# A transformer block on one core: the key and query stacks of groups 1 to 3 put together through DRAM

## What is computed

```python
q = (src @ Wq + bq).reshape(B, T, 16, 8)          # 16 heads of 8 dimensions
k = (src @ Wk + bk).reshape(B, T, 16, 8)
v = (src @ Wv + bv).reshape(B, T, 16, 8)
scores = einsum('bqhd,bkhd->bhqk', q, k) * 8 ** -0.5
probs = softmax(scores)
attn = einsum('bhqk,bkhd->bqhd', probs, v).reshape(B, T, 128) @ Wo + bo
x = layer_norm(src + attn)
# then: each token goes to one of 4 experts by its router key, and a second layer norm
```

## Time and profile before

| | us |
|---|---|
| median of 3 timed runs | 369.08 |
| lowest and highest | 367.32, 375.83 |
| the profiled execution's own time | 369.33 |
| its span, first to last instruction | 367.5 |
| PE, DVE, ACT, POOL busy | 272.2, 247.6, 191.5, 145.1 |
| TensorE's mean granted clock, as a share of full speed | 0.878 |

### The profile page before, as it was taken

One profiled execution on the slowest core, in us unless ns is written; L12 is line 12 of the kernel. 1 busy time (PEld: TensorE's weight loads), 2 busy tenths in 40 slices (PEclk: granted clock), 3 DMA queues, 4 the chain that ended last, 5 costly groups with the idle time before them and its releaser, 6 DMA issues. The chain is left out here.

```text
span 367.5 us, 7953 instructions
## 1 busy us (share of the span) xinstructions
PE 272.2 (74%) x2807; PEld 197.3 (54%) x2807; DVE 247.6 (67%) x664; ACT 191.5 (52%) x357; POOL 145.1 (39%) x333
## 2 busy tenths in 40 slices
PE   2654686877876838759888888988865898679970
PEld 1233454545555524546557566756755757447860
DVE  5997788888888592263538656866864377728881
ACT  4323969979978764633654654465341233214420
POOL 1126547657557360131003301820420152726665
PEclk9966869989988985966999999999976699969995
DMA  5899910000000200000000000100120021242000
GB/s 152 239 332 336 320 61 0 1 2 0 0 3 2 110 4 2 0 0 2 2 2 4 3 2 2 61 4 0 62 75 0 2 90 31 73 125 58 25 23 19
DMA packets 19806, 20.46 MB, mean 56 GB/s; under 512 B 1554, under 2 KB 18224, under 8 KB 19640
## 3 DMA queue, kind: packets, MB, share of 16 engines
q1 hardware_dynamic: 18392, 16.77, 15.4%
q0 software_dynamic: 1376, 3.18, 2.5%
HBM read 7.85 MB, written 12.29 MB: 55 GB/s over the span
## 5 line engine op out<-in xcount | busy, mean ns | idle before, releaser
L1128 ACT ACTIVATE probs<-scores 128x1024 f32<-128x1024 f32 x32 | 32.8, 1025 | 54.7 <-PE scores L801 54.4
L1392 DVE TENSOR_REDUCE mneg<-scores 128x8 bf16<-128x1024 f32 x32 | 39.0, 1218 | 24.7 <-PE scores L794 22.2
L1256 DVE TENSOR_TENSOR_SCAN early<-a_both,bank 128x512 f32<-128x512 f32 x32 | 38.8, 1212 | 4.5 <-issue 4.0
L428 POOL TENSOR_SCALAR a_both<-early 128x508 f32<-128x508 f32 x32 | 19.6, 611 | 37.6 <-ACT early L1025 33.7
L1400 DVE RECIPROCAL sums<-bank 128x128 f32<-128x128 f32 x16 | 15.3, 957 | 23.5 <-PE bank L824 23.4
L648 PE MATMUL scores<-ident,early 128*128 128x128 f32 x64 | 16.6, 319 | 17.7 <-DVE early L1274 16.3
L609 PE MATMUL bank<-ident,early 128*128 128x128 f32 x136 | 25.3, 318 | 5.0 <-ACT h_fwd L1042 2.1
L801 PE MATMUL scores<-mnegT,pick 32*128 32x128 bf16 x256 | 27.8, 239 | 0.0
L453 POOL TENSOR_TENSOR ln_tmp<-ln_tmp,minus_half 128x8 f32<-128x8 f32 x16 | 26.4, 1650 | 1.3
L1025 ACT ACTIVATE early<-scores,gate_wT 128x512 f32<-128x512 f32 x28 | 19.9, 712 | 11.0 <-PE scores L635 3.7
L648 PEld LDWEIGHTS scores<-ident,early 128*128 128x128 f32 x64 | 10.2, 167 | 28.0 <-issue 28.0
(11 more groups left out here) (262 smaller groups left out, 797.8 us busy)
## 6 DMA issues: line engine op xcount, KB each, us to landing
sorted_rows<-blank SPq DMA_DIRECT2D x1, 8710.0 KB, 32.6
late<-sorted_rows SPq DMA_DIRECT2D x15, 130.0 KB, 2.1
x_rows<-in_x_dram SPq DMA_DIRECT2D x4, 256.0 KB, 3.4
w_s<-in_L_ffn_W_dram SPq DMA_DIRECT2D x1, 1024.0 KB, 6.2
w_s<-in_L_ffn_W_dram SPq DMA_DIRECT2D x4, 256.0 KB, 6.8
a_both<-in_L_ffn_b_dram SPq DMA_DIRECT2D x1, 1024.0 KB, 4.7
x_rows<-sorted_rows SPq DMA_DIRECT2D x4, 130.0 KB, 2.0
ctx_rows<-in_ctx_dram SPq DMA_DIRECT2D x1, 256.0 KB, 2.9
```

The source lines that it names most:

```text
L428: pool.tensor_scalar(a_buf[d][:, (k // 2) % 2, :, keep], tiles(keep_buf[:, i, :])[:, :, keep], CLAMP_HI, CLAMP_LO, ALU.min, ALU.max).then_ ...
L1128: act.activation(probs[:, n % 2, 1 - h::2, :].rearrange("p (j i) q -> p j i q", i=2), exp_banks.rearrange("p i j q -> p j i q"), ACT.Exp, ...
L1256: dve.tensor_tensor_scan(out_s, a, b, 0.0, ALU.mult, ALU.add).then_inc(s["s_ready"], 1)
L1392: dve.tensor_reduce(mneg[:, n % 2, h::2, 0:4], max_banks, AX.X, ALU.max, negate=True).then_inc(s["mx_r"], 1)
```

## The change

For groups 1 to 3 no selection products and no copies are made. SP, between L395 and L399, issues for each group and for keys and queries: two 256 KB writes of the hi part and two of the lo part into a DRAM tensor laid out as the stack is; a wait until the four have landed; and one load of the whole stack (1 MB) into SBUF. Each row moved is 2 KB. `score_step` waits for these two loads in place of the ACT copies. Group 0 keeps its products and copies.

```diff
+        k_spread, q_spread = (nc.dram_tensor(n, [NG - 1, NHEAD // 4, P, CHUNK], F32) for n in ("key_stacks", "query_stacks"))
...
+            def spread_rows(g, dram, whole, rest, whole_at, rest_at, whole_r, rest_r, out, into, stacks):
+
+                spread = dram.ap()[g - 1].rearrange("j (i b d) c -> b (j i) d c", i=4, b=4)
+                for src, planes, ready in ((whole, whole_at, whole_r), (rest, rest_at, rest_r)):
+                    sp.wait_ge(s[ready], g + 1)
+                    for b in planes:
+                        sp.dma_start(spread[b], src[:, :].bitcast(F32)).then_inc(s[out], 16)
+                sp.wait_ge(s[out], 16 * 4 * g)
+                sp.dma_start(stacks[g % 2][:, :, :].bitcast(F32), dram.ap()[g - 1].rearrange("j p c -> p j c")).then_inc(s[into], 16)
+
+            for g in range(1, NG):
+                if g == 1:
+                    sp.wait_ge(s["h_ready"], LAYERS * STEPS)
+                else:
+                    sp.wait_ge(s["st_p"], HALVES * TPC * (g - 1))
+                spread_rows(g, k_spread, k_hi, k_lo, (0, 1), (2, 3), "k_hi_r", "k_lo_r", "k_out", "k_in", k_st)
+                spread_rows(g, q_spread, q_hi, q_lo, (0, 2), (1, 3), "q_hi_r", "q_lo_r", "q_out", "q_in", q_st)
...
             def fusion(g, dst=bank[6]):
                 if g:
-                    pe.wait_ge(s["qs_act"], 4 * g)
+                    pe.wait_ge(s["q_lo_r"], g)
...
             def turn_fusion(g, dst=bank[7]):
                 pe.wait_ge(s["fus_s"], g + 1)
+                wait(pe, "k_lo_r", g)
...
                     if t1 == 0:
-                        pe.wait_ge(s["ks_act"], 4 * (g1 + 1))
-                        pe.wait_ge(s["qs_act"], 4 * (g1 + 1))
+                        pe.wait_ge(s["k_in"], 16 * g1)
+                        pe.wait_ge(s["q_in"], 16 * g1)
...
-                if t == 2 and g < NG - 1:
-                    stack_queries(g + 1)
...
-                if t == 1 and g < NG - 1:
-                    stack_keys(g + 1)
...
             def key_cols(g, src=bank[7]):
                 act.wait_ge(s["k_p"], g + 1)
+                wait(act, "k_out", 16 * 4 * (g - 1))
...
             def query_cols(g, src=bank[6]):
                 act.wait_ge(s["q_p"], g + 1)
+                wait(act, "q_out", 16 * 4 * (g - 1))
...
-                if t == 2 and g < NG - 1:
-                    query_stacks(g + 1)
...
-                if t == 1 and g < NG - 1:
-                    key_stacks(g + 1)
```

More of the change, by code:

```diff
@@ L233, in build @@
         blank_r blanked consts cum_r rank_p place_r scattered0 scattered1 scattered2 scattered3 steer_r
+        k_out k_in q_out q_in
         xsT_p xs_r hid_p hid_r hidT_p relu_r y_p acc_r acc_p acc_rs_r o_r dve2""".split()
@@ L725, in queries, with stack_keys, stack_queries @@
                 pe.matmul(dst[:, :], wq_s[:, :], xnT[:, :], start=True, stop=True).then_inc(s["q_p"], 1)
-            def stack_bank(g, j):
-                return bank[j] if g == 0 else bank[7 - j % 2]
-            def stack_keys(g):
+            def stack_keys():
                 for j in range(4):
                     if j == 0:
[L734 to L738, removed]
+                        pe.wait_ge(s["k_lo_r"], 1)
+                        pe.wait_ge(s["q_lo_r"], 1)
                     for lo, src in enumerate((k_hi, k_lo)):
-                        last = pe.matmul(stack_bank(g, j)[:, :], sel[:, lo, j, :], src[:, :], start=(lo == 0), stop=(lo == 1))
+                        last = pe.matmul(bank[j][:, :], sel[:, lo, j, :], src[:, :], start=(lo == 0), stop=(lo == 1))
                     last.then_inc(s["ks_p"], 1)
-            def stack_queries(g):
+            def stack_queries():
                 for j in range(4):
[L746 to L751, removed]
+                    pe.wait_ge(s["ks_act"], j + 1)
                     for lo, src in enumerate((q_hi, q_lo)):
-                        last = pe.matmul(stack_bank(g, j)[:, :], sel[:, 2 + lo, j, :], src[:, :], start=(lo == 0), stop=(lo == 1))
+                        last = pe.matmul(bank[j][:, :], sel[:, 2 + lo, j, :], src[:, :], start=(lo == 0), stop=(lo == 1))
                     last.then_inc(s["qs_p"], 1)
@@ L882, in _ @@
             pe.wait_ge(s["mask_done"], 3)
-            stack_keys(0)
-            stack_queries(0)
+            stack_keys()
+            stack_queries()
             pe.wait_ge(s["bv_c"], 1)
@@ L1094, in query_cols, with key_stacks, query_stacks @@
                 act.wait_ge(s["q_p"], g + 1)
+                wait(act, "q_out", 16 * 4 * (g - 1))
                 act.activation(q_hi[:, :], src[:, :], ACT.Identity, bias=col(R_BQ)).then_inc(s["q_hi_r"], 1)
-            def stack_bank(g, j):
-                return bank[j] if g == 0 else bank[7 - j % 2]
-            def key_stacks(g):
+            def key_stacks():
                 for j in range(4):
-                    act.wait_ge(s["ks_p"], 4 * g + j + 1)
-                    act.activation(k_st[g % 2][:, j, :], stack_bank(g, j)[:, :], ACT.Identity).then_inc(s["ks_act"], 1)
-            def query_stacks(g):
+                    act.wait_ge(s["ks_p"], j + 1)
+                    act.activation(k_st[0][:, j, :], bank[j][:, :], ACT.Identity).then_inc(s["ks_act"], 1)
+            def query_stacks():
                 for j in range(4):
-                    act.wait_ge(s["qs_p"], 4 * g + j + 1)
-                    act.activation(q_st[g % 2][:, j, :], stack_bank(g, j)[:, :], ACT.Identity).then_inc(s["qs_act"], 1)
+                    act.wait_ge(s["qs_p"], j + 1)
+                    act.activation(q_st[0][:, j, :], bank[j][:, :], ACT.Identity).then_inc(s["qs_act"], 1)
             def value_rows(g):
@@ L1150, in _ @@
             affine(LAYERS - 1, STEPS - 1)
-            key_stacks(0)
+            key_stacks()
             act.activation(bv_cols[:, :], ident[:, :], ACT.Identity, scale=0.0, bias=col(R_BV)).then_inc(s["bv_c"], 1)
-            query_stacks(0)
+            query_stacks()
             act.activation(sums[:, 0:TPC], ident[:, 0:TPC], ACT.Exp)
```

## The result

| | kernel before | changed kernel |
|---|---|---|
| median of 4 runs | 370.90 us | 396.65 us |
| lowest, highest | 367.32, 375.83 | 394.36, 398.77 |
| profiled execution, span | 369.33, 367.5 | 394.36, 392.6 |
| granted clock | 0.878 | 0.830 |

The ratio is 1.076, with a 95% interval of 1.072 to 1.081. The forecast was 383 with a range of 373 to 396: the direction was right, but the loss is 25.7 us where 13.8 were expected, and the median lies just above the range. The ratio compares runs in the faster of two states only, and by it the loss is about 28 us.

The account below looks back on a forecast made before the run. The attention was taken as bound by the round of PE, DVE and ACT, tile after tile. Saving 12 us but waiting for late stacks nets 5.1 lost; low clock adds 8.7: 13.8 on 369.33, predicted 383 us, range 373 to 396.

Parts of the forecast that it names:

- The removed work: Attention round, groups 1 to 3: closing key gap (2.44) and query gap (1.52) saves 4.0 us a group, 12 in all.
- When the stacks are there: SP's DMA chain: query stack lands 17.0 us after `k_hi`, later than the present score step by 1.9, 1.6 and 1.6.
- the middle link: Chain from key load's issue to query load's: key load 4.7 us, then the query writes' bytes 2.7 queued behind it.
- The upper bound of 23: Slowest chain from `k_hi`: each megabyte 6.2 us, queued bytes 4.2, 23 in all, 6 more a group.
- Completion of writes to DRAM: The chain's two middle waits: completion may be late when the target is HBM; by the rows 0.4 us more each.
- Behind the wait: PE idles some 5.9 us per stall, then runs at half clock for 5.8: 2.9 lost a stall, 8.7 for three.
- The sum: Whole kernel: 5.1 us of late stacks plus 8.7 of low clock, 13.8 more, giving 383 us, 3.8% slower.
- Hidden transfers: Rival: stacks land in time, needing a chain of 11.1 us from `k_hi`; 12 us gained, 357 us; chance 5%.
- A clock that holds: Rival: PE stalls but its clock stays full, only 5.1 us lost, 374.2 us; chance 14%.
- Slow transfers: Rival: 6.2 us for each megabyte moved, 32 us more, 401 us; chance of more than 395: 10%.

Follow-up runs that it names:

- early_full: Changed kernel, but groups 1 to 3 use group 0's stacks (transfers unread, PE never waits for them), plus extra PE products in all groups' gaps; 351.18 us, ratio 0.954.
- before_fill: Kernel before with extra, unread PE products alone, in gaps at t = 0 and 3 and in the last group; 362.99 us, ratio 0.985.
- early: Changed kernel with all transfers, but groups 1 to 3 use group 0's stacks, so PE never waits for the transfers; 365.48 us, ratio 0.991 to before.
- keys_only: Kernel before with only the key stacks of groups 1 to 3 put together through DRAM, query stacks still on PE and ACT; 368.70 us, ratio 1.000.
- order: Changed kernel with SP issuing the key stack's load behind the four query writes, not ahead of them; 384.97 us, ratio 1.046 to before.
- queries_only: Kernel before with only the query stacks of groups 1 to 3 put together through DRAM; 382.95 us, ratio 1.034.
- after_fill: Changed kernel with extra PE products in the stalls and in PE's gaps of groups 0 to 2, none in the last group; 384.87 us, ratio 1.042 to before.
- warm: Changed kernel with 8, 10 and 8 extra PE products ahead of the waits for the stacks; 389.21 us, ratio 1.062 to before.

## Why the prediction was right in direction and short in size

**The removed work, 4.0 us a group.** Right as a length of path: the gaps closed to 1.39 and 1.81. Right as a worth only where the clock is kept: `early_full` is 11.8 below `before_fill` (362.99 to 351.18), 12 forecast; the interval of its ratio is 5 us to either side, and its fillers are not quite the same, so this agrees with the 13 us of gaps as well. Without fillers it was worth 4 (`early`), and the key half alone nothing (`keys_only`). The sentence that failed is "the eight ACT copies and sixteen products a group cost nothing outside these two gaps": they gave something. They kept PE at work between the score steps of t = 1 and t = 2; with fillers in their place the clock held, with the same transfers running.

**When the stacks are there.** This is the step that failed, a term of the sum that was mis-sized: 17.0 us from `k_hi`, measured 19.4, 21.5 and 20.2, so 10 us more over three groups. So the stalls were 27.5 us and not 17. By its parts: the key writes 5.3 to 5.6 for 4.8 (SP issues the last of the four some 1.9 us after the first, 0.6 us for each, and it lands 3.4 later); the last load 5.0 to 5.5 for 4.7; and the middle link 8.9 to 10.8 for 7.5. For that link I had added the bytes of the query writes at 387 GB/s to the time of the key load. In stretches of half a microsecond of group 1, almost nothing moves from the issue at 172.23 to 173.5, then the 2.1 MB take until about 180.5, 300 GB/s on the mean (98 to 123 up to 175.0, 348 to 414 from 177.0 to 180.0), and SP issues at 181.09. Why it starts so slowly stays open. `order` and `queries_only` show the same writes landing in 3 to 4 us when no megabyte is ahead of them. It was the link to look at longest: the prediction's order of issues was right, and that the order was itself a cost, 2.8 us a group of chain and 3.9 of time, was not seen. The upper bound of 23 held.

**Completion of writes to DRAM.** In group 2 nearly all bytes of the query writes had moved by 221, and SP was released at 223.5. The rows of that stretch, shown at the end, have traffic at the share of one engine until 223.0, so the wait past 221 is mostly bytes still moving, and half a microsecond at most is left behind them; in group 1 a trickle of 8 GB/s ends by 181.0 and SP issues at 181.09. The Trainium skill ("DMA: Bandwidth & Descriptors", Anatomy of one DMA), of DMAs issued by GpSimd, says that completion can be surprisingly late when the target is HBM. These rows, of DMAs issued by SP, show no such long delay.

**Behind the wait.** PE had nothing else, and the clock was at half behind each stall, as forecast. Its cost was put at 8.7, and that held: from first to second probs of t = 3 it took 6.25 (188.01 to 194.26), 6.95 and 4.95 us where it took 4.70, 4.69 and 2.77, and from PE's start to the first probs 0.7 more each time, 8.0 in all. What the forecast lacked is falls that no long stall precedes. ACT's rows above have one, 4.4 us from 197.47 to 201.84 where it took 2.8 before; another is 5.5 us from 255.10 to 260.58 where it took 3.4. They add some 4 us. `after_fill`, which has fillers for both kinds, is 11.8 below the changed kernel. The clock also fell early: 0.2 us into the first stall, at the very start of the second (218.3) and 0.3 us into the third (262.7). How much of that is the stall's and how much the short gaps' before it no run separates.

**The sum.** `after_fill` stands 15.0 above the kernel before (lateness net of the saved work: 5.1 forecast, 16 by the rows of the chain), and the changed kernel 11.8 above `after_fill` (clock: 8.7 forecast). That these two add up to the whole is no test, since both are differences to the same run. The rows give one: 27.5 of stalls less 13 of gaps closed, and 12 of clock, make 26.5, and from the last probs ahead of the change to the last of the attention it took 26.6 us more (169.35 to 314.03 for 173.94 to 292.02). The two profiled executions differ in other places too: the changed one reached `k_hi` 4.3 us earlier (166.01 and 170.28), ahead of any effect of the change, and took 3.1 us longer from its last probs to the end (78.6 and 75.5), with the clock at half until 320.8 where it was full from 291.5. In `warm`, `order` and `after_fill` that last part is 75.4 to 75.7, so I don't count it as the change's.

**Rivals.** Hidden transfers: needed 11.1 from `k_hi`; `keys_only` shows that the keys alone make it, at 10.8 to 11.7 with the score step at 12.5 or later, since the query products still stand ahead of it. A clock that holds: no; it was at half in and behind all three stalls. Slow transfers: a bit over half of the way there, 20.4 us on the mean between 17.0 and 23. That the time still came out within 1 us of the range is in part luck: the range had been set wide for slow transfers and reached 396, not for falls of the clock outside the stalls.

## To carry to other kernels

Work taken off PE is worth what it took on the path less what it did for the clock, so look, beside the path, at how many small gaps are left in a row where it stood; products of half a microsecond to one, into a free bank and put into the gaps, kept it here. A round trip through DRAM is a chain of landings: add up issue times and landings link by link, and don't issue a megabyte ahead of small writes that a later link waits for. Where one of two like transfers has slack and the other not, move only that one: keys through DRAM with fillers took 357.25 us, 2.7% less than the kernel before and 9.9% less than the changed one. Fillers alone are 1.5 of the 2.7% (`before_fill`).

## What was not expected of the hardware

**A fall of the clock without a stall.** In `keys_only` it fell at 206.6 with no gap on PE above 0.6 us in the 3 us before it. In the kernel before a gap of 1.05 us ahead of `turn_shift` at 193.4 left it full; in `keys_only` the clock fell 1.4 us behind the same gap (1.06 us, up to 188.20). So one gap by itself did not decide it here.

**A transfer ends with its last engine.** Stretches of the changed kernel in group 2, between the last query write (issued by 216.5) and the query load at 223.51 (POOL busy, PEclk, DMA share, GB/s):

```profile
219.00:220.00 1.00, 0.22 (x2) 0.50 1.03 387
...
221.00:221.50 0.50, 0.00 (x0) 0.50 0.06 25
...
222.00:222.50 0.50, 0.00 (x0) 0.50 0.06 25
```

From 387 GB/s it drops to 25 at a share of 0.06, one sixteenth, and stays there until 223.0: what one of the 16 engines would move, for some 2 us, with the others done. In groups 1 and 3 the link was 8.9 and 9.1, in group 2 10.8; the tail is about as long as the difference.
